# Small work of a slot moved behind its first pair of score products, and the last batch's second input load moved into the loop

## The chip, the cores and the metric

The kernel runs on one core of one Trainium2 chip. The metric is device time in microseconds (us) of one execution, as the median of the runs. All durations below come from one profiled execution of the kernel before, or from its timed runs.

## The reference

What is computed, cut to what matters (B = 4 batches, N = 1024 rows, D = 256, 16 heads of 16, 8 experts, 512 routed rows):

```
z   = layernorm(x)
zn  = layernorm(z) * ln_scale + ln_bias
q, k, v = heads(zn @ w_qkv)                       # 16 heads of 16
att = softmax(q @ k.T / 4)                        # 1024 x 1024 a head
x1  = x + layernorm(z + (att @ v) @ w_proj + b_proj)
y   = layernorm(x1)
sh  = layernorm(silu(y @ sw1.T + sb1) * (y @ sw2.T + sb2)) @ sw3.T + sb3
# rows (index_b, index_t) of sh: shared result and best expert's result, weighted
out = x1 + layernorm(sh with those rows replaced)
```

## The kernel before

**Slots.** The attention of one batch is 64 slots (`SL`), of all four 256 (`NS`). The loop has 271 slots (`SLOTS`): slot t = 64 w + tau makes the maxima of step t and the softmax of step e = t - 12 (`LEAD`), so the first twelve slots have no scores and the last fifteen no maxima. In a slot, TensorE does this, in this order (end of the tensor block, from L1011):

1. the slot's items, taken from the list `RING_AT[t]`;
2. two of four max products (`max_products`, L976: 48-row bf16 products of queries and keys, two side by side);
3. the scores of step e (`scores`, L994: 16 bf16 products of 48 or 50 rows in two groups, issued as eight);
4. the other two max products;
5. the value product of step e - 1 (`value_product`, L1008: four f32 products of 32 columns each, side by side).

I call the four max products a, b, c and d. VectorE reduces each of them to a row maximum (L1233). ScalarE makes the exponentials of the scores (L816, two a slot) and takes most items out of PSUM. The negated maxima of a unit of eight slots are transposed by the item mt (L1017), split by VectorE (L1241, L1243) and brought by four small transfers of the SP queue (L451) into two extra rows of the queries, where the scores of that unit read them.

**The ring.** Items and max products share three PSUM banks in a fixed round (`ring`, `RING`, `R_INDEX`). `open_r` (L872) lets the product with number i start when the one with number i - 3 has been taken out of its bank, by VectorE or by ScalarE:

```
def open_r(*key):
    i = R_INDEX[key]
    if i >= 3:
        by_act, n = TAKEN[RING[i - 3]]
        pe.wait_ge(ra_free if by_act else rv_free, n + 1)
    return ring[i % 3]
```

TensorE runs its program in order, so a wait there holds all that stands behind it. The score banks (`sbuf2`, two of them) are apart from the ring.

**Items.** They prepare the next batch and finish the last one beside the attention: z (four transposes of the normalized input, L887), qk and v (projections, L917 and L895), p (output projection), x (transposes), h, u (two transposes) and w (hidden layer). The lists `Z_AT`, `V_AT`, `P_AT`, `H_AT`, `MT_AT` and some ranges in `ring_order` (L55) give the slots. Up to two items stand in one slot, then mt is one of them. Slot 48 (`MT_LATE`) has mt behind the other item.

**VectorE in a slot.** It takes mt first, then does the extra work of the slot (statistics, gates, reciprocals), then a, b, c, d, and after every eighth slot the negated maxima (L1236).

**SP and POOL at the end.** Behind the loop SP loads the last batch's input a second time into x_sb (`load_x`, L355) and stores the third batch's output. POOL then makes the base of the last residual from it (`z_with_bias`, L549 and L576), behind three small steps. VectorE's first step on the last projection (`add_x1`, L1181) waits for that, and the reciprocals of the last softmax sums (`last_results`, L1213) stand behind it on VectorE.

Of the kernel before, what the change touches and what calls it, by code (L numbers as in the profile page):

```python
# [7 lines left out]
B, N, D = 4, 1024, 256  # L8
# [25 lines left out]
NS = B * SL  # L34
# [1 line left out]
SLOTS = NS + LEAD + 3  # L36

LEAD_V = (0, 1, 6, 7)
Z_AT = (14, 14)
V_AT = (22, 25, 51, 52)  # L40
P_AT = (19, 20, 21, 23)
H_AT = (44, 45, 47, 48)

MT_AT = (2, 10, 17, 25, 33, 41, 48, 57)
MT_LATE = 48

F_AT = ((4, 5), (0, 1))

# [6 lines left out]
def ring_order():  # L55


    at = {-1: [("z", 0, i) for i in (0, 2, 1, 3)] + [("qk", 0, c, h) for c in range(2) for h in range(NH)]}
    for t in range(SLOTS):
        w, tau = divmod(t, SL)  # L60
        e = t - LEAD
        fill = []
        if t in LEAD_V:
            fill.append(("v", 0, LEAD_V.index(t)))
        if w < B and 2 <= tau < 6:
            fill.append(("qk", w, 2 + (tau - 2) // 2, tau % 2))
        if w + 1 < B and Z_AT[w > 0] <= tau < Z_AT[w > 0] + 4:
            fill.append(("z", w + 1, tau - Z_AT[w > 0]))
        if w + 1 < B and tau in V_AT:
            fill.append(("v", w + 1, V_AT.index(tau)))  # L70
        if w + 1 < B and 33 <= tau < 37:
            fill.append(("qk", w + 1, (tau - 33) // 2, (tau - 33) % 2))
        if 1 <= w < B and tau in P_AT:
            fill.append(("p", w - 1, P_AT.index(tau)))
        if 1 <= w < B and 40 <= tau < 44:
            fill.append(("x", w - 1, tau - 40))
        if 1 <= w < B and tau in H_AT:
            fill.append(("h", w - 1, H_AT.index(tau)))
        if 1 <= w < B and 56 <= tau < 58:
            fill.append(("u", w - 1, tau - 56))  # L80
        if 1 <= w < B and 59 <= tau < 63:
            fill.append(("w", w - 1, tau - 59))
        mt = [("mt", t // 8 - 1)] if tau in MT_AT and 0 <= t // 8 - 1 < B * HU else []
        row = fill + mt if tau == MT_LATE else mt + fill
        if t < NS:
            row += [("max", t, j) for j in range(4)]
        at[t] = row
    last = B - 1
    at[SLOTS] = ([("p", last, i) for i in range(4)]
                 + [("x", last, 0), ("x", last, 2), ("h", last, 0), ("h", last, 1), ("x", last, 1), ("x", last, 3)]  # L90
                 + [("h", last, 2), ("h", last, 3), ("gate",), ("mh", 0), ("mh", 1), ("oh",), ("te", 0), ("tg",)]
                 + [("mw", i) for i in range(2)] + [("u", last, i) for i in range(2)] + [("te", 1)]
                 + [("w", last, i) for i in range(4)])
    return at
# [38 lines left out]
def build(nc, x, ln_params, w_q, w_k, w_v, w_proj, b_proj, index_b, index_t, sw12, sb12, sw3, sb3,  # L133
# [11 lines left out]
    with ExitStack() as ctx:  # L145
# [207 lines left out]
        def _(sp):  # L353
# [87 lines left out]
            for t in range(SLOTS):  # L441
                w, tau = divmod(t, SL)
                if tau in MT_AT and 0 <= t // 8 - 1 < B * HU:
                    u = t // 8 - 1
                    g, qh = u % HU // NH, u % NH
                    sp.wait_ge(rv_free, TAKEN["mt", u][1] + 1)
                    first = plane_of(g * GH, 1)
                    for par in range(2):
                        for j in range(2):
                            row = 64 * par + KR + j  # L450
                            sp.dma_start(qp[row:row + 1, qh, first:first + 2, :],  # L451
                                         mp[GH // 2 * QT * par:GH // 2 * QT * (par + 1), u % 2, j, :])\
                              .then_inc(s_mrow[u % 2], 16)
                for u in range(B * HU):
                    first = 8 * u + 8 + LEAD + (4 if u % HU == 0 else 1)
                    if t == first:
                        result_rows(u)
                    if t == first + 3 and u < B * HU - 1:
                        reciprocals_out(u)
                    if t == first + 4 and u < B * HU - 1:  # L460
                        reciprocals_in(u)
                if w < B and 12 <= tau < 24:
                    pack_step(w, 2, tau - 12)
                if w + 1 < B and 46 <= tau < 58:
                    pack_step(w + 1, 0, tau - 46)
                if 1 <= w < B and tau == 11:
                    if w + 1 < B:
                        sp.wait_ge(s_norm["z"], w + 2)
                    else:
                        sp.wait_ge(s_x1, w - 1)  # L470
                    load_x(w - 1)
                if 1 <= w < B and tau == 32:
                    sp.wait_ge(s_x1, w)
                    sp.dma_start(x1_tiles[w - 1, :, :, :], x1[:, :, :]).then_inc(s_x1st, 16)
                if tau == 33 and w + 2 < B:
                    if w == 0:
                        sp.wait_ge(s_norm["z"], 2)
                    load_x(w + 2)
                if 2 <= w < B and tau == 24:
                    sp.wait_ge(s_res, w - 1)  # L480
                    sp.dma_start(out_tiles[w - 2, :, :, :], hid[:, :, :]).then_inc(s_out, 16)

            last = B - 1
            sp.wait_ge(s_x1, last)
            load_x(last)
            sp.wait_ge(s_res, last)
            sp.dma_start(out_tiles[last - 1, :, :, :], hid[:, :, :]).then_inc(s_out, 16)
            sp.wait_ge(s_av, NS)
            sp.dma_start(we12, ew12.rearrange("(k p) e f -> p k e f", p=P)).then_inc(s_we, 16)
            sp.dma_start(we3, ew3).then_inc(s_we, 16)  # L490
# [10 lines left out]
        def _(pool):  # L501
# [129 lines left out]
            for t in range(SLOTS):  # L631
# [9 lines left out]
                if 2 <= w <= B and tau == (6 if w < B else F_AT[1][1]):  # L641
# [3 lines left out]
                    scaled(hid, hid, "f", 0, rstd["f"][:, 0, :], D).then_inc(s_norm["f"], 1)  # L645
                    pool.wait_ge(s_norm["f"], w - 1)
                    nc.gpsimd.tensor_tensor(hid[:, :, :], hid[:, :, :], x1[:, :, :], ALU.add).then_inc(s_res, 1)
                if 1 <= w < B and tau == 15:
                    z_with_bias(w - 1)
                if tau in D_AT:  # L650
                    kk, qh = divmod(D_AT.index(tau), NH)
# [27 lines left out]
                if 1 <= w < B and tau == 52:  # L679
# [6 lines left out]
            step(nc.gpsimd.memset(pick, 0.0))  # L686
            nc.gpsimd.affine_select(out=pick, in_=pick, compare_op=ALU.not_equal, fill=1.0, base=0,
                                    pattern=[[-1, E], [0, P]], channel_multiplier=1).then_inc(s_wide, 1)
            z_with_bias(B - 1)
            pool.wait_ge(s_pickb, 1)  # L690
            nc.gpsimd.memset(ohTb, 0.0).then_inc(s_clear, 1)
            for k in ("y", "x"):
# [31 lines left out]
        def _(sc):  # L724
# [80 lines left out]
            for t in range(SLOTS):  # L805
                w, tau = divmod(t, SL)
                e = t - LEAD
                for key in RING_AT[t]:
                    if by_act(key):
                        ring_item(key)  # L810
                for a in range(2):
                    if 0 <= e < NS:
                        if e >= 2 and a == 0:
                            sc.wait_ge(s_av, e - 1)
                        sc.wait_ge(s_full, 2 * e + a + 1)
                        nc.scalar.activation(prob[:, e % 2, 2 * a:2 * a + 2, :].rearrange("p g n -> p (g n)"),  # L816
                                             sbuf2[a][:, :], ACT.Exp, scale=0.25).then_inc(s_free, 1)
                if e % 8 == 0 and 0 < e <= NS:
                    u = e // 8 - 1
                    sc.wait_ge(s_av, 8 * u + 8)  # L820
                    if u >= NH:
                        sc.wait_ge(s_rows[u % NH], ROWS * (u // NH))
                    nc.scalar.activation(oT[:, u % 2, :], obank[:, :], ACT.Copy).then_inc(s_oT, 1)
                if 1 <= w < B and tau in (47, 50):
                    i = (tau - 47) // 3
                    sc.wait_ge(s_added["h"], 4 * (w - 1) + 2 * i + 2)
                    tanh(2 * (w - 1) + i, 4 * i, 4)

# [41 lines left out]
        def _(pe):  # L870
# [86 lines left out]
            for t in range(SLOTS):  # L957
# [40 lines left out]
                def value_product(v):  # L998
# [10 lines left out]
                                               prob[:, v % 2, i, :], start=(kt == 0), stop=(kt == NT - 1))  # L1009
                    ins.then_inc(s_av, 1)  # L1010

                for key in RING_AT[t]:
                    if key[0] == "mt":
                        u = key[1]
# [2 lines left out]
                        nc.tensor.transpose(dst[0:GH * QT, 0:P], nm[:, u % 2, :], ident[:, :]).then_inc(r_full, 1)  # L1017
                    elif key[0] not in ("max", "ot"):
                        ring_item(key)
                if t < NS:  # L1020
                    max_products(range(0, 2))
                if 0 <= e < NS:
                    scores(0)
                    scores(1)
# [119 lines left out]
        def _(ve):  # L1144
# [145 lines left out]
            ve.wait_ge(s_const, C_ALL)  # L1290
            for t in range(SLOTS):
                w, tau = divmod(t, SL)
                mt = [key for key in RING_AT[t] if key[0] == "mt"]
                if mt and tau != MT_LATE:
                    ring_item(mt[0])
                if tau in (2, 3) and w + 1 < B:
                    if tau == 2:
                        ve.wait_ge(s_xin, x_count("pre", w + 1))
# [27 lines left out]
                        reciprocals(u)  # L1326
                if w + 1 < B and tau == 35:
                    residual(w + 1, 0)
                if 1 <= w < B and tau in (48, 51):
                    n = int(tau == 51)  # L1330
                    gate_first(2 * (w - 1) + n, act[:, 4 * n:4 * n + 4, :], hid[:, 4 * n:4 * n + 4, 0:F])
                if 1 <= w < B and tau in (48, 52):
                    n = int(tau == 52)
                    gate_second(2 * (w - 1) + n, act[:, 4 * n:4 * n + 4, :], hid[:, 4 * n:4 * n + 4, F:2 * F])
                if 1 <= w < B and tau in (51, 52):
# [5 lines left out]
                    if i == 1:  # L1341
                        ins.then_inc(s_stats["u"], 1)
                for key in RING_AT[t]:
                    if not by_act(key) and (key[0] != "mt" or tau == MT_LATE):
                        ring_item(key)

            last = B - 1
# [198 lines left out]
```

## Time and profile before

| | |
|---|---|
| timed runs | 1031.47, 1032.19, 1032.92 us (median 1032.19) |
| profiled execution | 1030.68 us, of which the span of instructions is 1028.9 us |
| start, up to the first max product | 0 to 45 us |
| slots 0 to 11 (no scores) | 45 to 85 us |
| slots 12 to 255 | 85 to 862 us |
| slots 256 to 270 (no maxima) | 862 to 890 us |
| after the loop | 890 to 1029 us |
| TensorE, VectorE, ScalarE, POOL busy | 928.2, 800.1, 617.7, 353.0 us |

How to read it: the engines run side by side and wait for one another through semaphores. Busy shares alone say little. What counts is the time from the start of a slot on TensorE to the start of the next, and in each slot the wait that ended last.

### The profile page before, as it was taken

Reading aid. Unit: us, or ns where it says so; the run is one execution under the profiler, and the core shown is the slowest. Engines: PE = TensorE matmul, PEld = TensorE weight load, DVE = VectorE, ACT = ScalarE, POOL = GpSimd, SP = SyncE. Lnnn points to the kernel's source line nnn. Section 1 sums busy time; section 2 is a strip of 40 time slices with the busy share of each in tenths; the row PEclk is TensorE's granted clock in tenths of the full one; section 3 lists DMA queues with packets and bytes.
Section 4 is the critical chain, followed back from the end, with each engine's and each line's share of the span. In section 5 each row is a group of like instructions: output and inputs, shape, how many; then the busy total and the mean of one; then the engine's idle time right before and its main releaser. Section 6 shows DMA issues by size and latency. Waiting matters only on the chain.

```text
span 1028.9 us, 16451 instructions
## 1 busy us (share of the span) xinstructions
PE 928.2 (90%) x6180; PEld 369.3 (36%) x6180; DVE 800.1 (78%) x1566; ACT 617.7 (60%) x720; POOL 353.0 (34%) x472
## 2 busy tenths in 40 slices
PE   5289999999999999999999999999999999626984
PEld 3132333333244334333343343333323332215773
DVE  4188888998878888989879879789898895055765
ACT  3024777777776776777767767777677778501110
POOL 3061003001744251319743623166342234243022
PEclk9596999999999999999999999999999999957998
DMA  5905101430161304300721024006310000241001
GB/s 137 143 1 70 61 14 52 74 77 14 57 111 33 93 13 68 77 14 14 131 91 59 12 44 91 25 13 117 106 59 12 12 12 13 72 175 41 1 1 62
DMA packets 60612, 58.33 MB, mean 57 GB/s; under 512 B 19140, under 2 KB 49620, under 8 KB 60148
## 3 DMA queue, kind: packets, MB, share of 16 engines
q1 hardware_dynamic: 59124, 55.37, 24.0%
q10 hardware_dynamic: 1024, 0.85, 0.7%
q8 instruction: 49, 0.80, 0.4%
q0 software_dynamic: 384, 1.05, 0.3%
q14 instruction: 31, 0.25, 0.1%
HBM read 18.00 MB, written 9.17 MB: 26 GB/s over the span
## 4 chain that ended last, share of the span: by engine, by line
PE 80%; DVE 10%; DMA 3%; ACT 3%; POOL 2%; issue 2%; SPq 1%; ACTq 0%; DVEq 0%; POOLq 0%
PE obank L1008 23%; PE sc L994 20%; PE ring L976 15%; PE ring L895 10%; PE ring L917 5%; DVE mx L1233 5%; PE sc L1076 3%; PE ring L887 2%; DVE st L1151 2%; ACT prob L816 2%; DMA x_sb<-x 1%; DMA kp<-parts 1%; PE ring L1017 1%; POOL x L576 0%; POOL x L549 0%
## 5 line engine op out<-in xcount | busy, mean ns | idle before, releaser
L1233 DVE TENSOR_REDUCE mx<-ring 128x1 f32<-128x512 f32 x1024 | 634.4, 681 | 129.0 <-PE ring L976 127.4
L816 ACT ACTIVATE prob<-sc 128x1024 f32<-128x1024 f32 x512 | 495.8, 1021 | 115.0 <-PE sc L994 113.7
L994 PE MATMUL sc<-qp,kp 48*128 48x512 bf16 (+1 forms) x2048 | 273.7, 379 | 2.0 <-DMA qp<-mp 0.9
L1008 PE MATMUL obank<-prob,vaug 128*32 128x512 f32 x2048 | 273.6, 606 | 0.7 <-ACT prob L816 0.7
L976 PE MATMUL ring<-kp,qp 48*128 48x512 bf16 x1024 | 240.5, 389 | 32.0 <-issue 20.1
L976 PEld LDWEIGHTS ring<-kp,qp 48*128 48x128 bf16 x1024 | 74.7, 93 | 281.9 <-DVE mx L1233 177.4
L994 PEld LDWEIGHTS sc<-qp,kp 48*128 48x128 bf16 (+1 forms) x2048 | 99.1, 95 | 105.7 <-ACT prob L816 22.2
L603 POOL TENSOR_TENSOR resid<-qkf,parts 128x1024 f32<-128x1024 f32 x11 | 23.5, 2132 | 127.2 <-ACT parts L757 127.2
L589 POOL TENSOR_TENSOR hid<-hid,b 128x512 f32<-128x512 f32 x24 | 30.6, 1273 | 105.4 <-ACT hid L781 105.4
L597 POOL TENSOR_TENSOR yA<-yA,sums 128x512 f32<-128x512 f32 x15 | 19.6, 1308 | 136.0 <-DMA sums<-reciprocal_scratch 136.0
L1008 PEld LDWEIGHTS obank<-prob,vaug 128*32 128x32 f32 x2048 | 40.3, 108 | 65.2 <-issue 62.3
L609 POOL TENSOR_SCALAR parts<-resid 128x1024 bf16<-128x1024 f32 x14 | 14.7, 1050 | 114.0 <-DVE resid L1223 113.0
L895 PE MATMUL ring<-w,yT 128*128 128x256 f32 x192 | 50.9, 406 | 1.4 <-ACT yT L732 1.4
L895 PE MATMUL ring<-wp,yA 128*128 128x256 f32 x128 | 33.7, 412 | 19.9 <-DVE yA L1216 19.9
L755 ACT ACTIVATE qkf<-ring 128x512 f32<-128x512 f32 x32 | 19.1, 596 | 46.7 <-PE ring L917 45.3
L895 PEld LDWEIGHTS ring<-w,yT 128*128 128x128 f32 x192 | 35.7, 198 | 26.3 <-DVE mx L1233 15.1
L887 PE MATMUL ring<-ident,zn 128*128 128x128 f32 x128 | 22.5, 313 | 24.3 <-DVE zn L1167 12.2
L732 ACT ACTIVATE yT<-ring 128x512 f32<-128x512 f32 x16 | 9.4, 597 | 52.7 <-PE ring L887 52.7
L765 ACT ACTIVATE vaug<-ring 128x512 f32<-128x512 f32 x16 | 9.6, 597 | 50.1 <-PE ring L895 42.2
L895 PEld LDWEIGHTS ring<-wp,yA 128*128 128x128 f32 x128 | 24.8, 203 | 34.4 <-DVE yA L1216 20.3
L895 PE MATMUL ring<-wv,zT 128*128 128x256 f32 x128 | 33.3, 405 | 0.4 <-DVE mx L1233 0.4
L917 PE MATMUL ring<-zT,wk 128*128 128x512 f32 x64 | 31.6, 619 | 0.4 <-DVE mx L1233 0.4
(192 smaller groups left out, 771.7 us busy)
## 6 DMA issues: line engine op xcount, KB each, us to landing
kp<-parts SPq DMA_DIRECT2D x96, 128.0 KB, 4.6
qp<-parts SPq DMA_DIRECT2D x180, 64.0 KB, 2.8
x_sb<-x SPq DMA_DIRECT2D x7, 1024.0 KB, 6.2
out<-hid SPq DMA_DIRECT2D x4, 1024.0 KB, 4.6
yA<-oT SPq DMA_DIRECT2D x126, 32.0 KB
sums<-reciprocal_scratch SPq DMA_DIRECT2D x31, 128.0 KB
x_scratch<-x SPq DMA_DIRECT2D x3, 1024.0 KB, 4.5
qp<-mp SPq DMA_DIRECT2D x128, 2.0 KB
```

Of the source, the lines that this page charges most:

```text
L589: nc.gpsimd.tensor_tensor(hid[:, t, :], hid[:, t, :], {"h": b12, "w": b3}[kind][:, :] .rearrange("p (o d) -> p o d", o=1).to_broadcast([P, ...
L603: nc.gpsimd.tensor_tensor(resid[:, :], qkf[:, :], parts[:, c % 2, 0, :], ALU.subtract)\
L816: nc.scalar.activation(prob[:, e % 2, 2 * a:2 * a + 2, :].rearrange("p g n -> p (g n)"), sbuf2[a][:, :], ACT.Exp, scale=0.25).then_inc(s_f ...
L887: ins = nc.tensor.transpose(dst[:, t * P:(t + 1) * P], src[:, 4 * h + t, kk * P:(kk + 1) * P], ident[:, :])
L895: ins = nc.tensor.matmul(dst[:, (t - 2 * i) * D:(t - 2 * i + 1) * D], src[:, k, t * P:(t + 1) * P], w[:, k, :], start=(k == 0), stop=(k == ...
L917: ins = nc.tensor.matmul(dst[:, :], w[:, k, mt * P:(mt + 1) * P], zT[:, k, h * HALF:(h + 1) * HALF], start=(k == 0), stop=(k == KD - 1))
L976: nc.tensor.matmul(dst[:, :], qp[rows, qh, h, qt * P:(qt + 1) * P], kp[rows, h, kh * HALF:(kh + 1) * HALF], start=True, stop=True).then_in ...
L994: ins = nc.tensor.matmul(dst[:, j * HALF:(j + 1) * HALF], kp[rows, h, kt * P:(kt + 1) * P], qp[rows, qh, h, :], start=plane == 0, stop=pla ...
L1008: ins = nc.tensor.matmul(obank[i * VW:(i + 1) * VW, :], vaug[:, b % 2, kt, c0:c0 + VW], prob[:, v % 2, i, :], start=(kt == 0), stop=(kt == ...
L1076: ins = nc.tensor.matmul(expert_bank(i)[:, t, :], lhs[:, m], w, start=False, stop=stop, skip_group_check=True)
L1151: ins = nc.vector.bn_stats(st6[k == "z"][:, t, :], src[:, t, 0:width])
L1233: nc.vector.tensor_reduce(mx[:, u % 2, n:n + 1], src[:, :], AX.X, ALU.max).then_inc(rv_free, 1)
```

## The change

In every slot a and b now stand ahead of the items, and c and d stay where they were: the new order on TensorE is a, b, mt, other item, scores, c, d, value product. The list `RING_AT` has the same order, and so the numbers of the ring have it too. VectorE takes a, b and mt, then does the extra work of the slot, then takes c and d. mt moves from place 10 to 9, `MT_LATE` is gone, the items z of the second and third round go to the places 9, 10, 16 and 17, and a tanh and a gate step come one slot earlier. The second load of the last batch's input is issued at place 0 of the slots after the last maxima, POOL's `z_with_bias` of that batch at place 2, and the store of the third batch's output at place 11.

```
-Z_AT = (14, 14)
+Z_AT = ((14, 15, 16, 17), (9, 10, 16, 17))
-MT_AT = (2, 10, 17, 25, 33, 41, 48, 57)
-MT_LATE = 48
+MT_AT = (2, 9, 17, 25, 33, 41, 48, 57)
...
-        if w + 1 < B and Z_AT[w > 0] <= tau < Z_AT[w > 0] + 4:
-            fill.append(("z", w + 1, tau - Z_AT[w > 0]))
+        if w + 1 < B and tau in Z_AT[w > 0]:
+            fill.append(("z", w + 1, Z_AT[w > 0].index(tau)))
...
-        row = fill + mt if tau == MT_LATE else mt + fill
-        if t < NS:
-            row += [("max", t, j) for j in range(4)]
-        at[t] = row
+        pairs = [[("max", t, j) for j in js] if t < NS else [] for js in ((0, 1), (2, 3))]
+        at[t] = pairs[0] + mt + fill + pairs[1]
...
@@ SP
+                if w == B and tau == 0:
+                    sp.wait_ge(s_x1, B - 1)
+                    load_x(B - 1)
+                if w == B and tau == 11:
+                    sp.wait_ge(s_res, B - 1)
+                    sp.dma_start(out_tiles[B - 2, :, :, :], hid[:, :, :]).then_inc(s_out, 16)
...
-            sp.wait_ge(s_x1, last)
-            load_x(last)
-            sp.wait_ge(s_res, last)
-            sp.dma_start(out_tiles[last - 1, :, :, :], hid[:, :, :]).then_inc(s_out, 16)
@@ POOL
-                if 1 <= w < B and tau == 15:
+                if 1 <= w <= B and tau == (15 if w < B else 2):
                     z_with_bias(w - 1)
...
-            z_with_bias(B - 1)
@@ ScalarE
-                if 1 <= w < B and tau in (47, 50):
-                    i = (tau - 47) // 3
+                if 1 <= w < B and tau in (46, 50):
+                    i = int(tau == 50)
@@ TensorE
+                if t < NS:
+                    max_products(range(0, 2))
                 for key in RING_AT[t]:
...
-                if t < NS:
-                    max_products(range(0, 2))
                 if 0 <= e < NS:
@@ VectorE
-                mt = [key for key in RING_AT[t] if key[0] == "mt"]
-                if mt and tau != MT_LATE:
-                    ring_item(mt[0])
+                for key in RING_AT[t]:
+                    if key[0] == "max" and key[2] < 2 or key[0] == "mt":
+                        ring_item(key)
...
-                if 1 <= w < B and tau in (48, 51):
+                if 1 <= w < B and tau in (47, 51):
...
-                if 1 <= w < B and tau in (48, 52):
+                if 1 <= w < B and tau in (47, 52):
...
-                    if not by_act(key) and (key[0] != "mt" or tau == MT_LATE):
+                    if key[0] == "max" and key[2] >= 2:
                         ring_item(key)
```

## Rows read from the trace of the kernel before

**Rows 1.** The page: the chain that ended last, share of the span by engine.
```profile
PE 80%; DVE 10%; DMA 3%; ACT 3%; POOL 2%; issue 2%; SPq 1%; ACTq 0%; DVEq 0%; POOLq 0%
```

**Rows 2.** The chain, 413 to 428 us: start, length, what. Slots 116 and 120.
```profile
413.25 1.92 PE ring L895 x8
415.17 0.32 PE ring L976 x2
415.49 0.87 PE sc L994 x8
416.37 0.30 PE ring L976 x2
416.66 0.99 PE obank L1008 x8
...
425.13 0.59 PE ring L887 x4
```

**Rows 3.** Timeline of slot 147 (item p0): start, length, engine; in brackets idle before.
```profile
510.87 0.39 PE L976 MATMUL ring<-kp,qp 48*128 48x512 bf16 x2
511.10 1.03 PE L994 MATMUL sc<-qp,kp 48*128 48x512 bf16 x8
511.29 2.49 DVE L1233 TENSOR_REDUCE mx<-ring 128x1 f32<-128x512 f32 x4 [1.93 <-PE ring L976]
512.04 0.09 PEld L976 LDWEIGHTS ring<-kp,qp 48*128 48x128 bf16 x1 [0.19 <-DVE mx L1233]
512.36 1.06 PE L1008 MATMUL obank<-prob,vaug 128*32 128x512 f32 x8
513.36 1.99 PE L895 MATMUL ring<-wp,yA 128*128 128x256 f32 x8
```

**Rows 4.** The chain again, 428 us: a slot with mt and transposes, its end.
```profile
428.21 0.21 PE ring L1017
...
431.59 0.32 PE ring L976 x2
```

**Rows 5.** The chain, slot 41 with mt alone, and the start of slot 42.
```profile
176.26 0.21 PE ring L1017
...
179.15 0.32 PE ring L976 x2
```

**Rows 6.** Timeline of slot 4, before any scores: an item behind the four products.
```profile
62.57 2.48 DVE L1233 TENSOR_REDUCE mx<-ring 128x1 f32<-128x512 f32 x4 [1.20 <-PE ring L976]
...
63.91 0.30 PEld L917 LDWEIGHTS ring<-zT,wq 128*128 128x128 f32 x2 [0.51 <-DVE mx L1233]
```

**Rows 7.** Timeline of slots 0 and 1: first products, then item v1.
```profile
45.15 1.00 PE L976 MATMUL ring<-kp,qp 48*128 48x512 bf16 x3 [20.07 <-issue]
...
47.19 3.78 PE L895 MATMUL ring<-wv,zT 128*128 128x256 f32 x8
```

**Rows 8.** Timeline of ScalarE and of TensorE: the last qk item of slot 133.
```profile
472.19 1.92 ACT L816 ACTIVATE prob<-sc 128x1024 f32<-128x1024 f32 x2
...
469.01 1.98 PE L917 MATMUL ring<-zT,wq 128*128 128x512 f32 x4
```

**Rows 9.** Timeline, slot 76: scores that wait for the rows of maxima.
```profile
278.85 1.05 PE L994 MATMUL sc<-qp,kp 48*128 48x512 bf16 x8 [0.91 <-DMA qp<-mp]
```

**Rows 10.** The chain behind the loop, 891 to 913 us.
```profile
891.85 2.04 SPq L389
...
900.70 4.31 POOL x L549 x8
...
909.68 0.70 DVE x L1181
...
911.17 1.76 DVE sums L1213
```

**Rows 11.** Timeline: POOL's last residual of the loop (873 us), first p item.
```profile
873.59 4.55 POOL L647 TENSOR_TENSOR hid<-hid,x 128x2048 f32<-128x2048 f32 x1
...
889.86 3.72 PE L895 MATMUL ring<-wp,yA 128*128 128x256 f32 x16
```

## The prediction

> **What bounds the kernel now.** I read the page's chain first: TensorE holds 80% of it, VectorE 10% [rows 1]. Then I read the chain through the loop, slot by slot. A slot without items is 0.32 + 0.87 + 0.30 + 0.99 = 2.48 us, all TensorE; a projection adds 1.92 in front (slot 4.41) [rows 2]. So where a slot has an item, its cost is what it takes on TensorE, and what matters is whether an item can start as soon as TensorE comes to it.
>
> The timeline of one item slot gives the ring's delays [rows 3]. The pair a, b starts at 510.87; VectorE's four reductions start 0.42 later and last 2.49. One lasts 0.69, so the others follow at steps of (2.49 - 0.69) / 3 = 0.60. a is reduced at 511.98, and the weights of d, which waits for a's bank, load at 512.04: a bank is free 0.06 after its reduction. From d to the value product are 0.32, from there to the next slot 1.00. The scores start 0.23 into the slot and take 0.87 [rows 2], so TensorE comes to c at 1.10, but d starts at 1.17: 0.07 of waiting. VectorE ends with d at 513.78, that is 0.42 *after* the next slot has begun at 513.36. This lag costs nothing today, since an item at the head of the slot waits for the bank of b, reduced long before.
>
> **The change part by part.**
>
> *An item behind a and b.* The number of the ring is now ... c, d, a, b, item. The item takes the bank of the d of the slot before. That is free 0.42 + 0.06 = 0.48 into the slot [rows 3]; behind a and b alone the item could start at 0.32 [rows 2]. So it waits 0.16, and a wait on TensorE holds scores and the rest. That such a wait is real is seen before the first scores, where items stand behind the four products: reductions start at 62.57, b's ends at 62.57 + 0.60 + 0.68 = 63.85, and the weights of the item load at 63.91, released by VectorE [rows 6]. The slot becomes 0.48 + 1.92 + 0.87 + 0.32 + 0.99 = 4.58 against 4.41. The 0.32 there holds a gain: c and d go as a pair without waiting for a (0.07 less than today), and it is in the sum. After an item slot VectorE's lag is the same within 0.02 (d's reduction ends 0.42 + 0.60 + 0.69 = 1.71 behind c, the next slot starts at 0.32 + 0.99 = 1.31, free at 0.46). I take 0.16. By the lists, 79 slots from slot 12 on have one item and no mt (slot 48 apart): 79 x 0.16 = 12.6 us. The bounds are 0.12 and 0.20 an item, 9.5 to 15.8.
>
> The pair a, b takes 0.32 behind a product of another shape, the pair c, d behind the scores 0.30 with 0.07 of waiting in it [rows 2, 3]: about 0.10 goes with the change of shape. The Trainium skill, TensorEngine Tiling (Array Packing), section Key Properties, says that changing the tiling mode, not just the tile, drains TensorE; the change adds one such switch a slot (pair to item). By that rule alone an item costs about 0.10 more and gets 0.07 back, 0.03 net, and no bank would matter; by the rows the switch is hidden in the wait of 0.48.
>
> *mt and another item.* The order is a, b, mt, item, c, d. mt starts at 0.48; the item takes the bank of a, which is free at 0.42 + 0.69 + 0.06 = 1.17 [rows 3]. With a projection the slot is 1.17 + 1.92 + 0.87 + 0.32 + 0.99 = 5.27 against 4.41 (today mt hides the load of weights, so it costs 0.02 beside a projection; I count 0): + 0.86, in 9 slots, 7.7 us. With transposes, 1.17 + 0.59 + 2.18 = 3.94 [rows 2] against 431.59 - 428.21 = 3.38 [rows 4]: + 0.56, in 11 slots (17, 41, 57, and the new 9 of two rounds), 6.2 us. Bounds: the wait could be 0.1 shorter or 0.1 longer, 11.9 to 15.9 for both.
>
> *mt alone.* d now takes the bank of b, free at 0.42 + 0.60 + 0.69 + 0.06 = 1.77; the slot is 1.77 + 0.32 + 0.99 = 3.08 against 179.15 - 176.26 = 2.89 [rows 5]. + 0.19 in 4 slots, 0.8 us. In two more slots of the last round VectorE's extra work is longer than TensorE's, before and after: 0. Moving z to 9 and 10 takes one slot with mt alone and one with z apart (2.89 + 3.08) and makes one with both and one without (3.38 + 2.48, the difference to 3.94 is counted above): - 0.1 in two rounds, - 0.2. Slot 48: mt no longer stands right behind the negated maxima, but h3 behind it waits for a; I take 0, within 1 us for the four of them.
>
> *VectorE's extra work* moves from before a to between b and c. Behind b TensorE does the item and the scores, and a slot with a projection still leaves VectorE the 1.93 idle it has today [rows 3]; the slots in which it is too much for TensorE stay too long by the same amount. 0, cover: the projection. Without it the price is the work itself, 0.6 to 1.3 a slot.
>
> *ScalarE.* A qk item keeps ScalarE 1.23 before the exponentials. Today these end at 472.19 + 1.92 = 474.11, 5.10 behind the start of the item [rows 8]. The next slot starts 1.92 + 0.87 + 0.32 + 0.99 = 4.10 behind the item instead of 4.41, and its second half of scores 0.23 + 0.43 later, at 4.76. It waits until 5.15: 0.39, of which 0.07 is today's wait of d. + 0.33 in the six slots that follow a last qk, 2.0 us (0 to 3).
>
> *Start of the loop.* v0 is done today while TensorE waits 20 us for the first keys; now it stands behind a and b of slot 0. Then it takes 3.7 at the clock of that stretch, as v1 does today [rows 7], and the slots up to 7 keep their period (item 1.92, then 0.42 + 0.60 + 0.69 + 0.06 = 1.77 for two reductions, 3.69 in both orders [rows 6]). The second item comes 3.7 + 0.6 + 1.77 = 6.1 behind 45.2, at 51.3 against 47.2, but in the faster clock, so the third comes at 55.0 against 52.8 (47.2 + 3.7 + 1.9). At the end of the stretch two reductions less stand behind the last item: - 1.2. Sum + 1.1 (0 to 3).
>
> *The maxima rows one slot earlier.* The scores of slot 76 wait 0.91 for the DMA of mt [rows 9]; the transfer starts 2.5 us earlier: - 0.9. On SP that mt now stands ahead of the reciprocals' fetch in the same slot, which so goes out some 7 us later; POOL's product with it is needed by the p items ten slots on: 0.
>
> *The tail.* Today SP issues the second load of x behind the last result rows (891.85 + 2.04 = 893.89), POOL gets it at 900.70 and needs 909.68 - 900.70 = 8.98, VectorE adds x1 at 909.68 and only then makes the last reciprocals at 911.17 [rows 10]. In the new order the load goes out near 862 ahead of SP's last mt and of the last two units' rows (0.6 us of SP time, none of which was late), POOL starts when its last residual ends, at 873.59 + 4.55 = 878.1 [rows 11], and is ready at 887.1. One product with the sums (1.3) stands behind it on POOL, done at 888.4, before TensorE needs it at 889.86 [rows 11]; if that cover of 1.5 were gone, the p items would shift by the excess. POOL's three small steps end near 891. Next comes VectorE's first add, once p0 is done near 892, over before 894. The last result rows become the end: SP issues them until 893.89 [rows 10]. When they land is not shown, since nobody waits for it. It is after 893.9 and before 900.7, where the 1 MB load issued behind them was there; they are 32 to 128 KB, so I take the early third, 896.0. (The Trainium skill, DMA: Bandwidth & Descriptors, section Anatomy of one DMA, puts the fixed cost of a DMA on the GpSimd path at about 2.0 us; by that it would be 896.2 and the sum the same.) The reciprocals start at 896.0 instead of 911.17: - 15.2 (- 10.5 to - 17.3). The store of the third batch's output leaves near 880, with nothing due behind it until 890.
>
> *The sum.* 12.6 + 7.7 + 6.2 + 0.8 - 0.2 + 2.0 + 1.1 - 0.9 = + 29.3 in the loop, - 15.2 behind it: + 14.1. The profiled execution took 1030.68 (span 1028.9 and 1.8 around it), so 1044.8 for it. The median of the runs is 1.5 above that execution, so 1046.3, and I say 1046.
>
> **The rivals.**
>
> *The bank is free in time.* Should d's bank be free when TensorE comes to the item (if reductions of the new order ran ahead, with VectorE idle 1.93 us in each item slot), only the switch remains: 99 x 0.03 = 3, plus 2.0 + 1.1 - 0.9 elsewhere, is + 5, and with the tail - 10: 1022. It decides from 0.14 us less lag on VectorE. For it: VectorE is idle in these slots. Against it: that idle time comes before c, and d's end follows from c's start, whatever VectorE did earlier.
>
> *The tail gives less.* If the last rows land later beside the 3 MB of expert weights that are issued behind them, or another step becomes last, 10 us instead of 15: 1051 (rows landing near 900.7). For it: the rows' landing is not shown, as nobody waited for it. Against it: they are issued first.
>
> *The clock.* Were the granted clock to fall to its lower level in a stretch of waits in the loop, as it does in the slots before the scores, every slot there is near twice as long; ten of them cost some 20 us: 1066. Against it: TensorE is busy over 85% of the new slots.
>
> *The change does nothing in the loop* (the ring is kept filled in another order than the list says): not possible by the code, since list and program change alike.
>
> **How the numbers follow.** Forecast 75%, bank free 12%, tail 7%, clock 3%, a loop and a tail that cancel within 0.2% 3%. The forecast's own bounds, its terms taken together, are 1039 to 1053 (9.5 to 15.8, 11.9 to 15.9, 0 to 3 twice, 1 for slot 48, 2 for the tail). The tail's rival at 1051 lies inside. I add 3 us below, for waits counted twice where slots of both kinds meet: 1036 to 1053. 0.2% is about what a measurement of this kernel can tell from no change: faster 12%, same 3%, slower 85%.
>
> **What would show it.** In the profile after: weights of items (L895, L917, L887) released by VectorE 0.48 into the slot, and 1.17 behind mt; item slots of 4.58, 5.27, 3.25 and 3.94; d issued with c in item slots; slots without items unchanged at 2.49; 0.3 lost behind the last qk; slots 12 to 255 together 28 us longer. Behind the loop, no wait of VectorE for POOL L576, and L1213 within 6 to 7 us of the end of the loop. Item slots at 4.41 or below would make the forecast wrong, and so would a wait longer than 8 us ahead of L1213.

## The result and the profile after

The changed kernel takes 1047.91 us (median of four runs, 1045.65 to 1048.84) against 1031.83 for the kernel before beside it. The ratio is 1.0155 with a 95% interval of 1.0136 to 1.0175, so it is slower by 16.1 us, or 1.6%. Its profiled execution has a span of 1045.4, 16.5 more than before. I set the slots of the two traces side by side. A slot is counted from the end of the work of the slot before it on TensorE, so that a wait at its head is its own (for slots 8 and 12, with no value product ahead of them, from 0.30 behind the start of d). Slot 8 starts 1.2 later than before, slots 12 to 255 take 30.4 more, the loop ends 31.6 later, and behind it 15.1 are given back. The forecast for the profiled execution was + 29.3 and - 15.2.

The page of the changed kernel, its chain by engine. It answers to [rows 1], where VectorE held 10%.

```profile
PE 66%; DVE 23%; ACT 4%; issue 3%; DMA 2%; POOL 1%; ACTq 1%; SPq 0%; POOLq 0%; DVEq 0%
```

The chain through slot 84 of the changed kernel (start, length, what). It answers to [rows 2].

```profile
310.76 0.04 issue
310.80 1.99 PE ring L894 x8
312.80 0.98 PE sc L993 x8
313.77 0.26 PE ring L975 x2
314.04 1.29 DVE mx L1232 x2
315.32 0.14 issue
315.46 1.97 PE ring L894 x8
```

This is the new bound, a circle of five steps: item, scores, the pair c and d, their two reductions on VectorE, and the next item, which waits for d's bank. It is 1.99 + 0.98 + 0.26 + 1.29 + 0.04 = 4.56 us. The value product and the pair a, b have left the chain; they now fit into the time of the reductions. In the kernel before the chain of such a slot was TensorE alone, 4.41.

The timeline of slot 34 in the changed kernel (in brackets idle before), which answers to [rows 3].

```profile
155.99 2.00 DVE L1232 TENSOR_REDUCE mx<-ring 128x1 f32<-128x512 f32 x3
156.28 0.39 PE L975 MATMUL ring<-kp,qp 48*128 48x512 bf16 x2
156.73 0.30 PEld L916 LDWEIGHTS ring<-zT,wk 128*128 128x128 f32 x2 [0.36 <-DVE mx L1232]
```

The first of the three reductions is d of the slot before. It ends near 156.67, and the item's weights load at 156.73, 0.45 into the slot that began at 156.28; 0.48 was forecast.

The chain where mt and v1 stand in one slot (25), and where the scores follow the last qk item:

```profile
128.45 0.69 DVE mx L1232
129.14 0.04 issue
129.19 1.99 PE ring L894 x8
...
488.61 1.93 ACT prob L815 x2
490.53 0.05 issue
490.58 0.61 PE sc L993 x4
```

The slot begins at 128.01 and v1 starts at 129.19, 1.18 into it, behind the reduction of a. In the lower three lines the second half of the scores stands until ScalarE's late exponentials end, as forecast.

The chain behind the loop, which answers to [rows 10]. No step of POOL is left in front of the reciprocals; the last rows are the end, and the reciprocals start 6.4 behind the loop's end at 921.47, where before it was 911.17 - 889.85 = 21.3.

```profile
923.46 4.34 DMA yA<-oT
927.80 0.02 issue
927.83 1.76 DVE sums L1212
```

SP's timeline has the issue of these rows:

```profile
922.86 2.62 SPq L387 DMA_DIRECT2D yA<-oT  x2
```

### The profile page after: what moved, and what is told of

Same layout as the page of the kernel before. It is cut to its first block, busy times and chain, and to the rows that moved or that the text cites. A ratio compares the mean times of both kernels' runs of the same rounds, so it can differ in the third digit from the quotient of the medians.

```text
span 1045.4 us, 16450 instructions
## 1 busy us (share of the span) xinstructions
PE 938.6 (90%) x6178; PEld 361.8 (35%) x6180; DVE 810.0 (77%) x1566; ACT 615.3 (59%) x720; POOL 352.3 (34%) x472
## 4 chain that ended last, share of the span: by engine, by line
PE 66%; DVE 23%; ACT 4%; issue 3%; DMA 2%; POOL 1%; ACTq 1%; SPq 0%; POOLq 0%; DVEq 0%
PE sc L993 18%; DVE mx L1232 18%; PE obank L1007 14%; PE ring L975 11%; PE ring L894 10%; PE ring L916 5%; PE sc L1075 3%; ACT prob L815 2%; PE ring L886 2%; DVE st L1150 1%; DMA qp<-parts 1%; ACTq L801 1%; ACT qkf L754 1%; DMA x_sb<-x 0%; DMA yA<-oT 0%
## 5 line engine op out<-in xcount | busy, mean ns | idle before, releaser
L1232 DVE TENSOR_REDUCE mx<-ring 128x1 f32<-128x512 f32 x1024 | 645.9, 682 | 154.3 <-PE ring L975 150.6
L975 PE MATMUL ring<-kp,qp 48*128 48x512 bf16 x1024 | 225.6, 387 | 31.0 <-DMA qp<-parts 22.3
L975 PEld LDWEIGHTS ring<-kp,qp 48*128 48x128 bf16 x1024 | 65.3, 93 | 314.6 <-DVE mx L1232 161.3
L993 PEld LDWEIGHTS sc<-qp,kp 48*128 48x128 bf16 (+1 forms) x2048 | 90.0, 95 | 132.7 <-issue 40.6
L780 ACT ACTIVATE hid<-ring 128x512 f32<-128x512 f32 x24 | 14.3, 597 | 37.2 <-PE ring L894 37.2
```

The costliest lines, as they stand in the source:

```text
L975: nc.tensor.matmul(dst[:, :], qp[rows, qh, h, qt * P:(qt + 1) * P], kp[rows, h, kh * HALF:(kh + 1) * HALF], start=True, stop=True).then_in ...
L993: ins = nc.tensor.matmul(dst[:, j * HALF:(j + 1) * HALF], kp[rows, h, kt * P:(kt + 1) * P], qp[rows, qh, h, :], start=plane == 0, stop=pla ...
L1232: nc.vector.tensor_reduce(mx[:, u % 2, n:n + 1], src[:, :], AX.X, ALU.max).then_inc(rv_free, 1)
```

## The experiments

**The two parts alone.** First the kernel before with only the end's moves:

```
+                if w == B and tau == 0:
+                    sp.wait_ge(s_x1, B - 1)
+                    load_x(B - 1)
+                if w == B and tau == 11:
+                    sp.wait_ge(s_res, B - 1)
+                    sp.dma_start(out_tiles[B - 2, :, :, :], hid[:, :, :]).then_inc(s_out, 16)
...
-                if 1 <= w < B and tau == 15:
+                if 1 <= w <= B and tau == (15 if w < B else 2):
                     z_with_bias(w - 1)
```

> The kernel before with only the moves of the last batch: its input loaded at place 0 behind the last maxima, the base of the last residual at place 2, the third batch's output stored at place 11. The order in a slot stays old. My theory (the end needs nothing of the new order in the slots): 15.1 less than before, about 1016.7, slots 12 to 255 unchanged within 0.5. Rival (the last result rows land early only because the new loop leaves SP and the DMA queues free at that point): 10 less or fewer, 1022 or more.

Measured: 1017.58, ratio 0.9876 (0.9844 to 0.9908). The chain:

```profile
893.37 4.01 DMA yA<-oT
...
897.40 1.76 DVE sums L1214
```

The loop ends at 891.37 and the reciprocals start 6.03 behind that, against 6.4 in the changed kernel. What stands behind the loop takes 123.0 instead of 139.0: - 16.0, so the gain of the end needs nothing of the new order. Slots 12 to 255 took 2.4 more here, against the 0.5 I had allowed. Slots 51 to 53 of the last round alone took 2.6 more; the last section takes them apart. Then the changed kernel with the old end:

> The changed kernel with the old place of the three moves, so only the order in the slots is changed. My theory (the two parts are independent): 31 more than before, about 1063. Rival (part of the loop's loss is contention with the earlier load and store): 1058 or less.

Measured: 1062.57, ratio 1.0306 (1.0275 to 1.0338). Slots 12 to 255 take 807.49, the same as in the changed kernel to the hundredth. The moved load leaves behind slot 255, at 893.41 in the changed kernel, so only the last fifteen slots could suffer from it; they take 27.9 in both kernels and in the kernel before. The parts add up, and the loop's loss is none of the earlier load's.

**Is it the bank of d?** The reductions were made shorter in both orders; the maxima leave out a quarter of the keys:

```
-nc.vector.tensor_reduce(mx[:, u % 2, n:n + 1], src[:, :], ...)
+nc.vector.tensor_reduce(mx[:, u % 2, n:n + 1], src[:, 0:384], ...)
```

> The kernel before, with the row maxima taken over 384 of the 512 columns of each max product (a quarter of the keys is left out of them). VectorE's reductions are shorter, some 0.55 each and 0.47 apart. My theory (TensorE sets the slots, VectorE's lag costs nothing in the old order): a slot with a projection 4.33 instead of 4.41 (the wait of d for a's bank is gone), one without item unchanged at 2.48 or 0.06 less; 10 to 20 less than before in all. It is the base for the narrow kernel in the new order.

> The changed kernel, with the same narrow row maxima (384 of 512 columns, a quarter of the keys left out of them). My theory (an item waits for d's bank): that bank is now free some 0.2 into the next slot, before TensorE comes to the item at 0.32, so a slot with one item is 4.43, 0.10 over the narrow kernel in the old order and not 0.16 to 0.25; mt with a projection still waits for a's bank, free at about 1.03, and is 0.7 over it. Slots 12 to 255 together 20 to 23 over the narrow old order instead of 31. Rival (the price of an item behind a and b is the change of shape on TensorE, no bank matters): 31 over it, as with the full reductions.

Measured: 1006.27 and 1011.46, ratios to the kernel before of 0.9749 (0.973 to 0.9769) and 0.9806 (0.9778 to 0.9834). These kernels leave out work, so they are no versions to use. The first came out 25.5 under the kernel before, more than the 10 to 20 expected. Slots 12 to 255 take 757.2 and 775.8, a difference of 18.6 instead of 30.4, under the 20 to 23 expected and far from the rival's 31. Not all of the fall from 30.4 is the wait of items: up to slot 199 the difference is 18.2 instead of 26.2, and from slot 200 on, where VectorE's extra work of the last round lies, it is 0.4 instead of 4.2. A single item slot (qk1, slot 34) is 4.32 and 4.43, mt with a projection 4.34 and 5.15. The timeline of slot 34 in the new order, narrow:

```profile
149.91 0.55 DVE L1232 TENSOR_REDUCE mx<-ring 128x1 f32<-128x384 f32 x1
150.32 0.39 PE L975 MATMUL ring<-kp,qp 48*128 48x512 bf16 x2
150.64 0.30 PEld L916 LDWEIGHTS ring<-zT,wk 128*128 128x128 f32 x2 [0.23 <-DVE mx L1232]
```

d is reduced at 150.46, 0.14 into the slot, and the item starts at 0.32, when TensorE comes to it. (The releaser in brackets had long been done: the 0.23 is no wait for it.) The waits of the changed kernel and of its narrow form (engine, line, releaser: total us, times, longest):

```profile
PE ring L894 <- DVE mx L1232: 5.3, 25, 0.4
PE ring L916 <- DVE mx L1232: 3.6, 10, 0.5
```
```profile
PE ring L894 <- DVE mx L1232: 2.1, 6, 0.4
PE ring L916 <- DVE mx L1232: 2.9, 6, 0.5
```

With d's bank free in time, a plain single item slot costs 0.106 more than in the old order, in place of 0.159 (the mean of 51; slot 212, 1.1 shorter beside the last round's extra work, is left out). What it is can be read from starts. In [rows 3] the scores begin 0.23 behind the pair a, b; here the item begins 0.32 behind it. So a pair costs 0.09 more in front of an item than in front of scores, and the scores last 0.01 longer behind an item (0.88 against 0.87 from their start to that of c): 0.10, with hundredths lost in between. In the full kernel the pair's 0.32 lies inside the wait of 0.45, which is 0.22 over 0.23; with the 0.01 of the scores and 0.08 less in the pair c, d, where d no longer waits for a, it is 0.15 to 0.16, as measured. The narrow old order has no such wait of d to lose: its slots without items are 2.41, against 2.49.

The drain that the Trainium skill tells of (TensorEngine Tiling (Array Packing), section Key Properties: a change of tiling mode drains TensorE) has no figure there. The trace agrees with it, with 0.09 for pair to item; that these 0.09 are a drain, and not another cost of the same step, no run here separates.

**mt behind the other item.**

```
-        at[t] = pairs[0] + mt + fill + pairs[1]
+        at[t] = pairs[0] + fill + mt + pairs[1]
```

> The changed kernel, but where a slot has mt and another item, the other item comes first and mt behind it. So the item takes the bank of d and mt that of a. My theory (the second item waits for the bank of a, free at 1.17, and mt is the shorter one, which then has the item's time as cover): mt with a projection 4.8 instead of 5.28, with transposes 3.5 instead of 3.95, some 9 less than the changed kernel in all, 1039. Rival (the pair of items costs its length and its changes of shape whatever their order): within 1 of the changed kernel.

Measured: 1036.6, ratio 1.0045 (1.0026 to 1.0063) to the kernel before. The item of slot 25 now starts with d's bank and mt is short behind it:

```profile
126.94 1.99 PE ring L894 x8
128.94 0.11 PE ring L1018
129.05 0.97 PE sc L993 x8
```

mt with a projection is 4.70 instead of 5.29 (- 0.585 in each of nine), with transposes 3.57 instead of 3.95, and the three slots with h3 and mt lose 0.71 each. In all, slots 12 to 255 are 11.6 shorter, more than the 9 expected. So the wait for a's bank was real, and a matter of order only.

**Items behind the scores.** TensorE's two blocks change places, and ScalarE takes the items behind the exponentials:

```
-                for key in RING_AT[t]:
-                    if key[0] == "mt":
...
                 if 0 <= e < NS:
                     scores(0)
                     scores(1)
+                for key in RING_AT[t]:
+                    if key[0] == "mt":
...
```

> The changed kernel, but TensorE makes the items (mt too) behind the scores of the slot instead of ahead of them, and ScalarE takes them behind the exponentials. Ring numbers stay. My theory (in the changed kernel an item waits 0.48 for d's bank and, behind mt, 1.17 for a's): behind the scores, 1.19 into the slot, both banks are free, so a single item slot is 0.32 + 0.87 + 1.92 + 0.32 + 0.99 = 4.42 instead of 4.57, mt with a projection 4.45 to 4.55 instead of 5.28, and nothing is lost behind the last qk: 24 less than the changed kernel, about 1024. Rival (the items' banks are freed later, since ScalarE takes them behind the exponentials, and hold the a of the next slot): 10 less or fewer, 1038 or more.

Measured: 1026.89, ratio 0.9955 (0.9939 to 0.997), 21.0 under the changed kernel. Slot 35:

```profile
161.22 0.32 PE ring L975 x2
161.54 0.87 PE sc L993 x8
162.41 1.91 PE ring L916 x4
164.32 0.32 PE ring L975 x2
```

With the value product of 0.99 behind it, it is all TensorE again, 4.42, and mt with a projection 4.45. No work was left out here, so this shows the bank's wait in the full kernel: 0.13 of the 4.56 was due to where the items stood, and an item behind the scores is 0.02 over the old order. It fell short of the 24 forecast where an item is short. Behind two z items in a row:

```profile
278.60 1.94 ACT prob L812 x2
280.53 0.68 ACT zT L731
...
281.26 0.39 PE ring L975 x2
```

ScalarE frees z's bank only behind the exponentials, and the next a waits: slot 75 takes 2.98 instead of 2.49. That is the rival's mechanism. It is not there behind projections, but behind all short items: together with the wait behind it, an item z or u costs 0.51 more than in the old order, x 0.33, and mt with transposes 0.20, some 10 us in all.

**One more wait on TensorE.**

```
                     elif key[0] not in ("max", "ot"):
+                        pe.wait_ge(s_made, 1)
                         ring_item(key)
```

> The changed kernel with one more wait on TensorE ahead of each item but mt, for a count that was reached long before. The items v0, p0, p2, h0, x0, u0 and w0 have such a wait of their own beside that for the bank, and their slots were 0.07 longer than those of items with the bank's wait alone. My theory (a wait more is a step more between the bank's release and the weights, 0.07 each, while TensorE has nothing queued): about 5 more than the changed kernel, 1053, the single item slots 4.64 instead of 4.57. Rival (satisfied waits cost nothing, these items are long for what they fetch): within 1 of the changed kernel.

Measured: 1054.57 (ratio to the kernel before 1.0213, 1.0194 to 1.0232), slots 12 to 255 together + 4.6. The 52 single slots with one wait grew by 0.062 each, the 15 whose item has a wait of its own by less than 0.001. The chain of a slot that had 0.04 between reduction and item:

```profile
156.77 0.61 DVE mx L1233
157.38 0.14 issue
157.52 1.96 PE ring L916 x4
```

The same 0.14 stands in front of 315.46 above, where p2 waits for its own input as well. A second wait delays the start behind the release by 0.06 to 0.10; a third adds nothing. Where TensorE does not stand idle for the bank, the second wait costs nothing either: in the narrow pair of kernels the slots with v0, p0, h0 and w0 are 0.106 apart, as the plain ones are.

**Reciprocals ahead of a.** In the changed kernel VectorE's `reciprocals(u)` was moved from between b and c to the head of the slot.

> The changed kernel, but VectorE makes the reciprocals of the softmax sums (once in eight slots) ahead of the reduction of a instead of between b and c. My theory (between b and c they push c and d back, so the bank of d is free later in the next slot, and the negated maxima end later): the slots with place 0, 8, 16 ... lose their extra: an item slot there 3.24 instead of 3.42, one without item 2.61 instead of 2.71, some 2.6 less than the changed kernel in all. Rival (these slots are long for the negated maxima alone): within 0.5 of the changed kernel. Second rival (ahead of a, the reciprocals push a and b back and so hold the second item of a slot): more than the changed kernel.

Measured: 1046.03, ratio 1.0141 (1.0116 to 1.0166) to the kernel before. The step between the scores and the value product of slot 32, first as changed, then with the reciprocals ahead:

```profile
149.49 0.52 PE ring L975 x2
```
```profile
151.37 0.42 PE ring L975 x2
```

Thirteen such slots without an item, the eight single item slots behind the reciprocals and one slot with mt lost 0.106 each, 2.3 in all. The three slots of place 15 in the later rounds (79, 143 and 207) gave 1.2 back: there the reciprocals, at the head of the slot, wait 0.4 for the transfer of their sums, and a stands behind them. That is the second rival's mechanism in three slots. With small gains against it, slots 12 to 255 came out 1.4 shorter, not 2.6. The timed difference to the changed kernel, 1.9, is between runs taken at different times and decides nothing by itself.

**The load alone.** As the first experiment, without the last two lines of its diff: POOL's `z_with_bias` stays behind its small steps.

> The kernel before with only the second input load of the last batch and the store of the third output moved into the loop; POOL's base of the last residual stays behind its small steps. My theory: POOL can start it when those steps end (886.7 in the trace before) and is done 9.0 later, near 895.8, just ahead of the landing of the last rows: the last reciprocals start 13.5 to 15 sooner than in the kernel before, the time is 1018 to 1019, and the place of POOL's step is worth 0 to 1.5. Rival (the step at place 2 is what brings the gain, since POOL's small steps and sums stand ahead): 10 less or fewer, 1022 or more.

Measured: 1019.5, ratio 0.9886 (0.9861 to 0.9912).

```profile
893.48 4.51 POOL x L578
...
898.09 0.70 DVE x L1183
```

The reciprocals start 8.2 behind the loop's end, not 6.0. POOL is last again: its small steps ended at 888.57, 2.8 ahead of the loop's end where I had 3.2, and the base took 9.4, not 9.0. So, by the start of the reciprocals, the load is worth 13.1, under the 13.5 to 15 expected, and the place of POOL's step 2.2, more than the 0 to 1.5 expected.

**A version that beats both.** Old order, the end's moves, and mt at the places 9 and 49:

```
-MT_AT = (2, 10, 17, 25, 33, 41, 48, 57)
+MT_AT = (2, 9, 17, 25, 33, 41, 49, 57)
```

> The kernel before, with the moves of the last batch, and the maxima rows (mt) one slot earlier at place 9 instead of 10 and at place 49 instead of 48 alone, not behind another item. The order a slot has stays old. My theory: the wait of 0.91 ahead of the scores of slot 76 goes, and the long slots 48 get shorter: 1014 to 1016, 1 to 2 under the kernel with the tail alone. Rival (what ended late next takes over: the transfer of another unit): the same as the tail alone within 0.5.

> The kernel in the old order with the earlier maxima rows and the moves of the last batch once more, on another chip, with more rounds, since its first run rests on one profile and three rounds. Expected: 1013 to 1015, 1.6 to 1.8% under the kernel before. If the loop's times between slots 12 and 255 were chance, another sum than 774.6 would show.

Measured: 1013.97, ratio 0.9841 (0.9809 to 0.9873), and again 1015.83, ratio 0.9848 (0.9822 to 0.9874); the second run lies over its own bound of 1015. Slots 12 to 255 took 774.57 (2.5 under before) and 776.57, with 1.8 of the 2.0 more in slots 51 to 53, where the clock fell. The wait of [rows 9] is gone (- 1.0). Three slots with h3 and mt behind it took 5.08 and the next 2.49; now h3's is 4.41 and mt's 2.89, - 0.27 each. In the first round, mt alone in slot 48 took 3.65, in 49 2.89 (- 0.65 with what slot 48 keeps, 2.60). The intervals of this and of the tail alone overlap, so the 2.5 rests on the traces.

## Why the prediction came out as it did

*What bounds the kernel* held: the loss came from where TensorE waits for a bank.

*Single items* were sized 12.6 (79 at 0.16). The traces give 52 at 0.158, 15 at 0.229 and 8 at 0.329, 14.3 in all (the other four stand in slots counted below). The wait itself was 0.03 shorter than I took, the scores behind an item 0.01 longer. Two surcharges were missing: the second wait of v0, p0, p2, h0, x0, u0 and w0 (0.06, shown by the extra wait), and in slots behind one with reciprocals a late d, because these stand between b and c on VectorE (0.106, shown by moving them). One reading was wrong, at no cost to the sum: I put about 0.10 for a change of shape into the pair a, b behind an item. By their starts the pair takes 0.23 there as in a slot without item; the 0.09 lies between pair and item.

*mt with a projection*: 7.7 forecast, 9 x 0.885 = 8.0 measured. *mt with transposes and the moved z* (6.2 - 0.2): nine slots gave 5.1 and the eight slots around the moved z 1.4, together 6.5. *mt alone*: 0.8 and 0.8. Waits for a's bank at 1.17: 1.18 read.

*Slot 48*: 0 forecast, + 0.6 measured; three slots with h3 and mt grew by 0.30, one with mt alone shrank by 0.34.

*VectorE's extra work at 0* is the step that failed. Its cover, the projection, exists only in item slots, and I wrote that slots in which it is too much stay as they are. But the reciprocals stand in slots without an item, between b and c, and hold back the negated maxima: thirteen slots behind them grew by 0.105, three at place 24 shrank by 0.03, 1.3 in all, beside the 0.9 in item slots above. Nor was the rest of that work at 0: in the last round slots 22 to 35 grew by 0.3, slot 207 shrank by 0.5 and slots 51 to 53 by 0.6, together - 0.8.

*ScalarE behind the last qk*: 6 x 0.30 = 1.8 against 2.0. *Slot 76*: - 1.0 against - 0.9. *Start of the loop*: + 1.2 against + 1.1 up to slot 8; in slots 12 to 14 0.8 came back. With a - 0.2 that is spread over the other slots in hundredths, the terms make the 30.4 of slots 12 to 255 within 0.1. That the loop missed its forecast by 2.3 only (31.6 against 29.3) is in part luck: the terms that I had too small or at 0 came to 4.5, and slots 12 to 14 and the last round, for which I had nothing, took 1.6 off.

*The tail*: - 15.1 against - 15.2. The last rows are issued until 922.86 + 2.62 = 925.48 and land at 927.80, 2.3 behind; I had taken 2.1 (893.89 to 896.0) as an estimate between bounds. The input's load left at 893.41, POOL's base began at 910.01 and its product with the sums was done at 920.2, ahead of the p items, as the order of the forecast has it.

*The rivals.* The bank free in time did not come: the item waits for d, as read from c's start. Its price of 0.03 an item was right, as the narrow pair shows (0.106, less the 0.08 of d's wait that the full old order has), but no kernel with full reductions met its condition. The one with the items behind the scores comes nearest, with 0.02 an item; it took 1026.89, not 1022, among other things because a waits behind short items for ScalarE. The point from which it decides, 0.14 us less lag, was met by the narrow reductions. The tail giving less did not come, and the clock did not fall in the loop of the changed kernel.

## What to carry to other kernels

A step that is moved later in a round of shared buffers takes the place of another in the release order, and its wait is read off as release time minus arrival time, both within the period; that gave 0.16 and 0.86 here to a few hundredths. Then look what else stands on the engine that releases the buffer: the reciprocals between b and c, put at 0, cost 2.2. Put the longest item where its buffer has been free for long, and a short one behind it: mt behind the item, or items behind the scores, took back 12 and 22 of the 30 us. When such a change is worth nothing and carries a part that is worth much, as the load of the last input was, measure the parts apart: the good one alone, with two places of mt, took 1.6% off in one run and 1.5% in the next.

## What the runs showed that I had not expected

A second wait in front of a TensorE instruction, long satisfied, costs 0.06 us when the engine stands idle for the first: 0.14 instead of 0.04 in the chain between release and work, and 4.6 us over the loop. A third is free.

TensorE's clock fell in the loop behind a pause. Windows around slots 51 to 53 of the last round (columns: window, its length, busy time of PE, PEld, DVE, ACT and POOL, granted clock, DMA share, GB/s) of the kernel with the tail alone, of the kernel before, and of the second run of the best version:

```profile
821.00:824.00 3.00, 0.58 (x6) 0.25 (x9) 3.00 (x8) 1.44 (x2) 0.49 (x1) 1.00 0.00 0
826.00:828.00 2.00, 2.00 (x12) 0.52 (x12) 2.00 (x7) 1.48 (x2) 1.06 (x6) 0.50 0.01 4
```
```profile
822.00:825.00 3.00, 1.43 (x10) 0.25 (x9) 3.00 (x9) 1.53 (x2) 1.41 (x1) 1.00 0.00 0
```
```profile
820.00:823.00 3.00, 1.43 (x14) 0.46 (x14) 2.52 (x7) 2.39 (x3) 1.26 (x1) 1.00 0.08 30
823.00:826.00 3.00, 3.00 (x19) 0.78 (x19) 2.97 (x9) 0.67 (x1) 0.07 (x1) 0.69 0.00 0
```

VectorE's extra work holds TensorE in all three. Behind the pause the granted clock stands at 0.50, the lower level of 1.2 GHz, for 6.8 us in the first and in the third (from 824.5 and from 824.1), and not at all in the second. The length of the pause alone does not decide it: TensorE is busy 0.58 of 3 us in the first, but 1.43 of 3 in both others. All five other kernels and runs in the old order show the fall (3.4 us long in the narrow one and in the first run of the best version), the kernel before does not, and none of those in the new order does. What decides stays open.

Slots 51 to 53 take 2.6 more in the kernel with the tail alone and 2.0 more in the second run of the best version, but only 0.2 more in its first. Of the 2.6, 0.9 is no matter of the clock: the pause itself is longer. VectorE's gate step stands in it, and POOL was already at work when the step began (timeline of the kernel with the tail alone, then of the kernel before):

```profile
820.22 1.26 POOL L599 TENSOR_TENSOR yA<-yA,sums 128x512 f32<-128x512 f32 x1 [6.74 <-DMA sums<-reciprocal_scratch]
820.50 1.53 DVE L1187 SCALAR_TENSOR_TENSOR act<-act,hid 128x512 f32<-128x512 f32 x1 [0.51 <-ACT act L786]
```
```profile
821.59 0.69 DVE L1186 SCALAR_TENSOR_TENSOR act<-act,hid 128x512 f32<-128x512 f32 x1 [0.50 <-ACT act L785]
821.65 1.76 POOL L597 TENSOR_TENSOR yA<-yA,sums 128x512 f32<-128x512 f32 x1 [7.08 <-DMA sums<-reciprocal_scratch]
```

The one that began second ran long: VectorE's 1.53 instead of 0.69 with 0.98 of POOL's step still to run, POOL's 1.76 instead of 1.26 with 0.63 of VectorE's to run. The load alone shows the first case again (1.50, begun 0.32 behind POOL). My third rival, priced for ten slots, thus exists, three slots long and in other kernels than the one forecast.
